# Two small router steps of a second attention, from VectorE to GpSimd

## The reference, cut to what matters

```python
x = x + xattn1(layernorm(x), ctx, ...)      # 16 heads of 8 channels, rotary, window of 64
h = layernorm(x)
scores = softmax(h @ gate_w.T, axis=-1)     # 8 values for each token
biased = scores + gate_b
_, idx = top_k(biased, 2)
w = take_along_axis(scores, idx, axis=-1)
y = sum of w * expert_idx(h), plus one shared expert for every token
x = x + y + z
```

## Time and profile before

| | |
|---|---|
| median of 3 runs | 695.95 us (694.52 to 699.04) |
| profiled execution, first to last instruction | 763.9 us |
| TensorE busy (share of the span) | 671.5 us (88%) |
| VectorE | 523.5 us (69%) |
| GpSimd | 504.9 us (66%) |
| ScalarE | 415.8 us (54%) |
| mean granted clock of TensorE | 0.953 of full speed |

### The profile page before, as it was taken

How to read it: one execution, slowest core, us unless ns; L and a number is a source line. 1 busy time by engine, 2 the same in 40 slices (tenths; PEclk the granted TensorE clock), 3 DMA queues, 4 the chain that set the end, 5 groups by cost and what they waited for, 6 DMA issues and landing times.

```text
span 763.9 us, 21054 instructions
## 1 busy us (share of the span) xinstructions
PE 671.5 (88%) x7092; PEld 546.5 (72%) x7092; DVE 523.5 (69%) x1515; ACT 415.8 (54%) x1158; POOL 504.9 (66%) x837
## 2 busy tenths in 40 slices
PE   8799998888876999999979999888888668788797
PEld 7567666665646999999957776666667568778787
DVE  5489988888663446555358898888886555555556
ACT  5477767654542434444447777656547445555563
POOL 5975788577564678877677778777667635455451
PEclk9899999999997999999979999999989989899999
DMA  5470000001331522343110101111211312222264
GB/s 166 124 305 2 17 27 27 27 30 36 137 99 48 160 70 81 97 127 89 46 36 29 30 26 40 54 37 37 66 34 37 89 51 77 61 75 72 75 232 152
DMA packets 45406, 57.78 MB, mean 76 GB/s; under 512 B 11379, under 2 KB 37142, under 8 KB 44630
## 3 DMA queue, kind: packets, MB, share of 16 engines
q1 hardware_dynamic: 36086, 38.17, 16.6%
q0 software_dynamic: 8640, 17.97, 7.1%
q10 hardware_dynamic: 576, 0.29, 0.1%
HBM read 33.82 MB, written 22.08 MB: 73 GB/s over the span
## 4 chain that ended last, share of the span: by engine, by line
PE 50%; POOL 17%; issue 12%; DVE 8%; ACT 5%; another core or an unknown queue 4%; DMA 2%; SPq 1%; DVEq 0%; POOLq 0%; ACTq 0%
POOL results L1625 9%; PE ptp L1349 8%; PE M L1366 7%; PE ptp L2078 6%; PE S L1326 5%; PE S L2059 5%; PE S L1330 3%; PE ptp L1352 3%; POOL xi L1618 2%; POOL rows L626 2%; PE M L1374 2%; PE M L1418 2%; PE S L2065 1%; SPq L707 1%
## 5 line engine op out<-in xcount | busy, mean ns | idle before, releaser
L626 POOL DMA_INDIRECT rows<-out_rows,posi x128 | 126.9, 991 | 50.1 <-issue 32.1
L806 ACT ACTIVATE pT<-ptp 128x512 f32<-128x512 f32 (+1 forms) x192 | 95.1, 525 | 97.7 <-PE ptp L1349 87.0
L1929 POOL DMA_INDIRECT results<-early,xs x71 | 69.0, 971 | 68.4 <-DVE early L2001 50.9
L1064 DVE TENSOR_REDUCE mx<-S 128x16 f32<-128x1232 f32 x64 | 91.3, 1427 | 18.3 <-PE S L1330 16.4
L1625 POOL DMA_INDIRECT results<-early,xi x71 | 75.9, 1069 | 40.5 <-DVE early L1687 35.1
L1065 DVE TENSOR_TENSOR pr<-S,mx 128x1232 f32<-128x1232 f32 x64 | 92.3, 1442 | 2.2
L1724 PE MATMUL S<-first_w,early 128*128 x568 | 77.2, 279 | 3.0 <-DVE early L1687 1.5
L1714 PE MATMUL S<-early,w1s 128*128 128x128 f32 x568 | 76.9, 279 | 0.6 <-ACT early L1659 0.6
L1366 PE MATMUL M<-pT,vm 128*32 128x128 f32 (+1 forms) x2048 | 74.7, 283 | 1.1 <-ACT pT L806 0.6
L1349 PE MATMUL ptp<-cst,pr 128*128 128x128 f32 x512 | 74.0, 290 | 0.0
L1724 PEld LDWEIGHTS S<-first_w,early 128*128 128x128 f32 x568 | 69.5, 193 | 5.9 <-issue 5.7
(11 more groups left out here) (221 smaller groups left out, 1527.9 us busy)
## 6 DMA issues: line engine op xcount, KB each, us to landing
xs<-rows SPq DMA_DIRECT2D x142, 66.0 KB
first_w<-in_e_W SPq DMA_DIRECT2D x2, 2048.0 KB, 8.2
swap<-results SPq DMA_DIRECT2D x32, 128.0 KB
first_w<-results SPq DMA_DIRECT2D x6, 512.0 KB
rows<-out_rows,posi POOLq DMA_INDIRECT x128
x_res<-in_x SPq DMA_DIRECT2D x1, 1536.0 KB, 8.4
W1r<-in_e_W SPq DMA_DIRECT2D x1, 1536.0 KB, 10.8
out_x<-x_res SPq DMA_DIRECT2D x3, 512.0 KB, 2.7
```

The lines of the kernel that those rows point to most:

```text
L626: nc.gpsimd.indirect_dma_start(rows[:, :], bass.IndirectOffsetOnAxis(posi[:, k, n:n + 1], 0), out_rows[:, ring_slot(groups, n), k, :], Non ...
L806: nc.scalar.activation(pT[0:rows_of, G * r:G * r + count, :], ptp[q % 2][0:rows_of, 0:count, :], ACT.Exp, scale=SCALE)\
L1064: do(V.tensor_reduce(mx[:, :].rearrange("p (g j) -> p g j", g=G), sc, AX.X, ALU.max))
```

## The change

VectorE keeps the sum and its reciprocal (`total_of`, which now keeps both halves apart and signals `total_ready` instead of waiting for itself). The multiplication by the reciprocal and the addition of the gate bias become GpSimd's: `softmax_logits` in `gpsimd`, behind the padded values of the same iteration and ahead of its scatters; for the last but one group in iteration 33 ahead of the scatter, for the last in iteration 35, ahead of the scatters there. `choose` waits for `keys_ready`. The two expert stages share the eight semaphores of `ys_out`, with counts that go on from the first to the second.

```diff
+    keys_ready, total_ready = (sem("keys_ready"), sem("total_ready")) if rope else (None, None)
...
+        def softmax_logits(g):
+
+            size = groups[g][1]
+            pg, kg, sums = prob[:, own_half(g), :], key[:, g % 2, 0:size, :], rtotal[:, own_half(g)]
+            pool.wait_ge(total_ready, g + 1)
+            steps.then(pool, nc.gpsimd.tensor_tensor(pg, pg, sums.unsqueeze(2).broadcast_to([128, size, E]), ALU.mult))
+            wait(pool, both_ready, g - 1)
+            nc.gpsimd.tensor_tensor(kg, pg, gb[:, :].unsqueeze(1).broadcast_to([128, size, E]), ALU.add).then_inc(keys_ready, 1)
+
...
                 if k >= 0 and live(n):
                     padded_values(n)
+            if rope and k in KEYS_AT[1]:
+                softmax_logits(KEYS_AT[1].index(k))
...
             if k == B + 1:
                 pool.wait_ge(rows_ready, B - 2)
+                if rope:
+                    softmax_logits(last_group - 1)
+            if rope and k == LT:
+                softmax_logits(last_group)
             if sends.get(k) and 1 <= k <= B:
                 pool.wait_ge(pv_done, k)
...
-        def softmax_logits(g):
-
-            size = groups[g][1]
-            pg, kg = prob[:, own_half(g), :], key[:, g % 2, 0:size, :]
+        def total_of(g):
+
             dve.wait_ge(prob_ready, g + 1)
-            do(V.tensor_reduce(total[:, 0:size], pg, AX.X, ALU.add))
-            do(V.reciprocal(rtotal[:, 0:size], total[:, 0:size]))
-            do(V.tensor_tensor(pg, pg, over_e(rtotal[:, 0:size], size), ALU.mult))
-            do(V.tensor_tensor(kg, pg, over_b(gb[:, :], size), ALU.add))
+            do(V.tensor_reduce(total[:, own_half(g)], prob[:, own_half(g), :], AX.X, ALU.add))
+            V.reciprocal(rtotal[:, own_half(g)], total[:, own_half(g)]).then_inc(total_ready, 1)
 
         def choose(g):
 
             b0, size, at, _ = groups[g]
             if rope:
+                dve.wait_ge(keys_ready, g + 1)
...
-                softmax_logits(KEYS_AT[1].index(k))
+                total_of(KEYS_AT[1].index(k))
...
-    ys_out = st["ys_out"][1]
+    ys_out = st["ys_out"]
...
+    def landings(s, tiles):
+
+        return first_use[s] + 16 * len(range(s, tiles, U))
+
...
-                    wait(dve, ys_out[i % U], 16 * (i // U))
+                    dve.wait_ge(ys_out[i % U], landings(i % U, i))
```

More of the change, by code:

```diff
@@ L641, in gpsimd @@
             pool.wait_ge(st["consts_in"], st["n_consts"])
-        sends = sent_in(layer)
+        sends, last_group = sent_in(layer), len(groups) - 1
         for k in [-4, -2] + list(range(-1, B + 6)) if rope else range(B + 6):
@@ L1195, in vector @@
             if step == "turn last but one" and rope:
-                softmax_logits(last - 1)
+                total_of(last - 1)
             if step in EARLY_STEPS and not rope:
@@ L1215, in vector @@
             if step == "softmax last" and rope:
-                softmax_logits(last)
+                total_of(last)
             if step == "choose last" and rope:
@@ L1557, in experts @@
     yp_ready, ys_ready = sem("yp_ready"), sem("ys_ready")
-    ys_out = st["ys_out"][0]
+    ys_out = st["ys_out"]
     w1_copied = st["w1_copied"] = sem("w1_copied")
@@ L1881, in load @@
             sp.wait_ge(ys_ready, before + 1)
-            sp.wait_ge(ys_out[before % U], 16 * (before // U) + 16)
+            sp.wait_ge(ys_out[before % U], landings(before % U, before + 1))
         at = row_of(sp, i) if row is None else row
@@ L1892, in results_stored @@
         for s in range(U):
-            sp.wait_ge(ys_out[s], 16 * len(range(s, tiles, U)))
+            sp.wait_ge(ys_out[s], landings(s, tiles))
     def combine(sp):
@@ L2191, in build @@
         st["scattered"] = [[ctx.enter_context(nc.semaphore(f"scattered{l}_{g}")) for g in range(LANES)] for l in range(2)]
-        st["ys_out"] = [[ctx.enter_context(nc.semaphore(f"ys_out{l}_{s}")) for s in range(8)] for l in range(2)]
+        st["ys_out"] = [ctx.enter_context(nc.semaphore(f"ys_out{s}_all")) for s in range(8)]
         rows = [nc.dram_tensor(f"rows{l}", (SHARED, RW), F32, kind="Internal").ap() for l in range(2)]
```

## The result

The median after is 704.08 us (701.06 to 707.82, 4 runs), before 695.39 us (694.52 to 699.04, 4 runs); the ratio is 1.0109 [1.0072, 1.0145], by which the change is about 7.6 us slower (the two medians are 8.7 us apart) where 0.6 us less, in effect no change, was forecast. The profiled execution after has a span of 699.3 us and an own time of 701.06 us. One execution of run 3 took 872 us; it is left out of that run's ratio, and since it is the one that was profiled, only an order is read from that run's trace.

A forecast was written before the change was run, and what follows sets the result against it. No one engine was taken to set the time; the chain passes between GpSimd, TensorE and VectorE. The terms -0.36 + 0.62 - 0.45 - 0.45 = -0.64 us, against a median of 695.95, gave 695.3 us, range 692 to 701.

The forecast's parts named there:

- k=10: Second attention's loop: VectorE, behind its input, can use about 0.36 us of what it drops; gain -0.36 us.
- k=14: Second attention's loop: GpSimd's two added instructions stand in front of the query sum that the scores need; +0.62 us.
- k=22: Second attention's loop: the dropped instructions lie on VectorE's chain; -0.45 us.
- k=28: Second attention's loop: again on VectorE's chain, GpSimd's part falling into its waits; -0.45 us.
- k=18 and 26: Second attention's loop: VectorE's gain and GpSimd's loss end in waits for TensorE; 0 each, 0.62 us each without cover.
- GpSimd's price: Each moved group on GpSimd: two instructions of 0.25 us, with dependency and handover 0.62 us, ends 0.48 and 0.76.
- the last group: Tail, iteration 35: choice 0, bounds -0.2 and +0.2; scatters 5.7 us later, covered by idle time before the first store.
- The rival of the late scatters: Tail: late scatters delay ScalarE or the first stores and all behind, up to +5.1 us, 701 us; chance 0.12.
- beyond 7 us slower: Whole kernel: needs both slow cases at once, 3.7 + 0.75 + 5.7 = 10 us; chance 0.04.
- GpSimd as the bound: Loop: without cover six groups pay 0.62 us each, three of them waiting too; +4.1 us, 700 us; chance 0.2.
- VectorE as the bound: Throughout: all nine groups give 0.45 to 0.5 us; -4.5 us, 691.5 us; chance 0.13.
- the shared memory interface: 18 new GpSimd instructions each stretch a VectorE instruction by 0.32 us; +5.8 - 0.6, 701 us; chance 0.03.

The follow-up runs named there:

- run 3: The kernel before with only the last group's multiply and add moved to GpSimd, the other eight groups on VectorE: 702.63 us, ratio 1.0095.
- run 10: The kernel before with only the groups of k = 10, 22 and 28 on GpSimd, the six others on VectorE: 695.24 us, ratio 0.9991.
- run 2: The changed kernel with the last group's multiply and add back on VectorE, the other eight groups on GpSimd: 694.75 us, ratio 1.0001.
- run 5: As run 2, but GpSimd still waits for the last reciprocal at the change's place, both products staying on VectorE: 700.72 us, ratio 1.0072.
- run 6: The changed kernel with the last group's two products between the fourth and fifth of iteration 35's eight scatters: 696.21 us, ratio 1.0000.
- run 7: The changed kernel with the last group's two products behind all eight scatters of iteration 35: 698.88 us, ratio 1.0053.
- run 9: The changed kernel with 22 slots instead of 16 for the rows that the second experts load: 698.03 us, ratio 1.0042.
- run 1: The kernel before, unchanged, timed and profiled anew: 696.1 us, ratio 1.0007, profile span 694.4 us.
- run 4: The kernel before with only the shared result counts of `ys_out` for both expert stages: 697.74 us, ratio 1.0016.
- run 8: The kernel before with five small powers added on GpSimd between its last scatter and first result store: 699.80 us, ratio 1.0067.

## Why the prediction was wrong, point by point

- **The sum over the loop** came out right by luck: -0.64 us forecast, -0.69 in these two profiles. Of its terms, k=10 gave -0.33 (forecast -0.36) and k=14 +0.65 over two periods (forecast +0.62). k=22 to 25 gave -0.71 and k=28 to 30 -0.78 where -0.45 each was taken. The zeros of k=18 and 26 were wrong: +0.45 from k=16 to 21, and by run 10 some -0.45 from the group of k=26. The errors cancel. And -0.69 is one end of a spread: the six traces with the changed loop (the change and runs 2, 5, 6, 7, 9) have 145.04 to 145.71 us, the three with the loop before (runs 1, 4, 8) 145.61 to 145.76, on average 0.25 us apart. In runs 2, 5, 7 and 9 it is 1.0 us, not 0.45, that is lost from k=16 to 21.
- **GpSimd's price** was right: 0.24 and 0.25 us for each product against the estimate of 0.25, and 0.56 us for the pair (443.19 to 443.50 + 0.25 at k=14) within 0.48 to 0.76. The rule in the Trainium skill (GPSIMD Engine Reference, "Engine selection"), about twice VectorE's time, isn't borne out at this size: 0.240 us against 0.192.
- **The failed step** is the last group: "2.6 us of cover are left, so 0. Without that cover up to 5.7." The mechanism stood there, with the last scatter 7.6 us later where 5.7 were forecast (its own terms give 617.0 us, so 5.4). That the first store is 5.7 us later too is chance: 7.6 less the 1.9 us of pause that went. The cover was not a property of the kernel: the 8.33 us of idle time came from an execution that was itself 68 us late, and ScalarE's hold of 7.70 us, which ended at 613.59, lay across it. In run 1 there is no such hold and the cover is 2.23 us. The prediction said that it couldn't see where those 68 us lay, used that doubt against the waits of k=18 to 30, and not in its sum against the one cover on which 5.7 us hung. Run 1's profile places them: of 69.5 us between the two spans 19.3 lie ahead of the scores of k=0, 7.1 from there to those of k=31, and 43.1 behind, where the cover stood. What made that execution long stays open.
- **The second failed step** is the price. The rival of the late scatters took the lateness over unchanged (5.7 - 0.6 = 5.1). The run of waits behind the store was not followed: eight pairs are loaded ahead, the ninth pair's rows wait for the first stores to land, TensorE stops, and the clock falls. In the tail that is 8.5 us instead of 5.7, in the timed runs 7.6. Runs 8 and 9 show both ends: late stores alone are enough, and with the slots opened 4.7 us return. By this price "beyond 7 us slower" did not need two slow cases at once, as the prediction had it; one was enough.
- **The place of the wait** was seen ("must wait there for the reciprocal"), but not that run 6's place existed in the same code, four scatters further on, where 5.8 of the 7.47 us of the wait are filled with work.
- **The choice on VectorE** waits 0.36 us for GpSimd's keys and comes 0.36 us later from the scores of k=31 (30.69 for 30.33), a little over the bound of 0.2:

```profile
564.62 0.37 DVE L997 MAX8 topv<-key 128x8 f32<-128x8 f32 x4 [0.36 <-POOL key L615]
```

In run 2, where both products are VectorE's, it comes at 30.81, so the difference can't be put down to the handover. The counts of `ys_out`: within the interval of run 4.
- **The rivals.** GpSimd as the bound, VectorE as the bound and the shared memory interface all fall with the loop's measured sum and with runs 2 and 3. The late scatters, at a chance of 0.12, were right in place, and low in price. Of the signs that were to show the forecast, the products' durations came, and the sixteen scatters in one row; the scores of k=16 are 0.34 us later counted from k=5, though 0.50 us earlier counted from k=0. Of the signs listed as "wrong would be", three came: the first result store late, VectorE idle in front of its last choice (0.36 us), and GpSimd's waits for the value products all but gone (0.3 us, for 2.7 in run 1). The last was meant for GpSimd as the bound and came without it.

## What to carry to other kernels

A step that must wait for another engine costs on an in-order queue what stands ready behind it, not what it takes itself: put it where the queue still has work to fill the wait with, or behind the last thing that is ready and not needed. An idle stretch is cover only if it is there in an execution as long as the timed runs; where the profiled one is longer, price the step without the cover. And follow a late store to the buffers that it frees: with sixteen slots the lateness came out, once, at tile 16, at one and a half times its size.

## What the runs showed of the hardware

- TensorE's granted clock fell from 1.00 to 0.50 (2.4 to 1.2 GHz) in a stretch of 5.60 us in which it had two transposes to do, and was 1.00 again from 602 us on; two groups of products ran at 0.50 (2.07 and 2.77 us for 1.06 and 1.50). It fell in the stops of runs 5 and 8 too (3.51 and 3.39 us between products, 0.50 from 596 to 598 us). With 1.09 us of idle time in the same place (run 9) it stayed at 1.00. So the stop of the changed kernel was charged 2.3 us on top. The Trainium skill (TensorE: Matmul & The Clock Gate, "What's actually happening") has the array fall to half rate when it is idle and come back with activity; the trace agrees (1.00, 0.50 behind the stop, 1.00 again).
- Indirect DMAs that wait for nothing follow each other on GpSimd at 1.26 to 1.27 us in most cases (0.96 us and 0.30 us of issue). With 71 result stores, 70 such steps are 89 of the 93.7 us from the first to the last store in the kernel before (run 1). TensorE has even less room there: it is busy for 14.00 of 14.00 us from 586 to 600.
